# Global attention in a four-layer kernel: four turned buffers, the weights' chain four steps farther ahead, six groups of scores, pixels normalised three steps before their products

## The reference

```
h = group_norm(x, gn_scale, gn_bias)
hf = h.reshape(B, N, C)
q = hf @ wq + bq
k = hf @ wk + bk
...
w_ = jax.nn.softmax(w_, axis=2)
o = jnp.einsum('bqk,bkd->bqd', w_, v)
o = o @ wo + bo
return x + o.reshape(B, H, W, C)
```

## Time and profile before

| what | value |
|---|---|
| median of 3 runs | 3576.88 us (3575.83 to 3576.98) |
| the profiled execution | 3578.49 us, span 3576.7 us |
| PE busy over the span | 3127.8 us (87%) |
| ACT busy | 2605.6 us (73%) |
| layer 1, first to last PV | 738 to 2336 us |

### The profile page before, as it was taken

One profiled execution on the slowest core, in us unless ns is written; L12 is line 12 of the kernel. 1 busy time (PEld: TensorE's weight loads), 2 busy tenths in 40 slices (PEclk: granted clock), 3 DMA queues, 4 the chain that ended last, 5 costly groups with the idle time before them and its releaser, 6 DMA issues. The chain is left out here.

```text
span 3576.7 us, 62857 instructions
## 1 busy us (share of the span) xinstructions
PE 3127.8 (87%) x20468; PEld 2095.9 (59%) x20468; DVE 2731.2 (76%) x6707; ACT 2605.6 (73%) x4733; POOL 2184.7 (61%) x2044
## 2 busy tenths in 40 slices
PE   7999998599998999899998999877898857788898
PEld 5777776366655666565665666555666623333338
DVE  5899998566666666666666666568799979998888
ACT  4778887377877877777877778759676567776764
POOL 5789886155555665565555656643023458887885
PEclk8999999799999999999999999989999956878789
DMA  8777774189995999789996999942354455666559
GB/s 220 200 199 206 200 197 121 29 165 190 196 181 109 196 198 195 146 152 185 196 188 121 185 186 192 196 124 101 120 181 159 169 168 169 195 196 192 172 187 289
DMA packets 1327541, 623.51 MB, mean 174 GB/s; under 512 B 1105520, under 2 KB 1207536, under 8 KB 1326448
## 3 DMA queue, kind: packets, MB, share of 16 engines
q1 hardware_dynamic: 1296448, 551.83, 68.3%
q0 software_dynamic: 29184, 67.27, 7.1%
q10 hardware_dynamic: 1584, 0.40, 0.1%
HBM read 184.48 MB, written 113.25 MB: 83 GB/s over the span
## 5 line engine op out<-in xcount | busy, mean ns | idle before, releaser
L1115 POOL TENSOR_TENSOR l_halves<-l_pr,l_halves 128x1024 f16<-128x1024 f32 x384 | 833.1, 2182 | 549.7 <-ACT l_halves L948 546.9
L1076 DVE CUSTOM_DVE_ANT_0 l_pr<-l_S,l_zero 128x512 f32<-128x512 f32 x1024 | 671.8, 685 | 236.2 <-PE l_S L781 234.8
L948 ACT ACTIVATE l_halves<-l_pr 128x1024 f16<-128x1024 f32 x512 | 515.1, 1047 | 258.1 <-DMA l_turned<-l_halves 257.1
L943 ACT ACTIVATE l_pr<-l_pr,l_st,l_cols 128x1024 f32<-128x1024 f32 x512 | 628.0, 1227 | 10.6 <-DVE l_st L1082 10.6
L863 PE MATMUL l_O<-l_turned,l_vh 128*128 128x256 f16 x2048 | 564.1, 275 | 74.7 <-DMA l_turned<-l_halves 73.6
L864 PE MATMUL l_O<-l_turned,l_vl 128*128 128x256 f16 x2048 | 562.7, 275 | 0.0
L865 PE MATMUL l_O<-l_turned,l_vh 128*128 128x256 f16 x2048 | 562.5, 275 | 0.0
L779 PE MATMUL l_S<-l_kh,l_qh 128*128 128x512 f16 x1024 | 394.5, 385 | 11.4 <-DVE l_st L1076 11.4
L780 PE MATMUL l_S<-l_kh,l_ql 128*128 128x512 f16 x1024 | 392.8, 384 | 0.0
L781 PE MATMUL l_S<-l_kl,l_qh 128*128 128x512 f16 x1024 | 392.1, 383 | 0.0
L2196 POOL TENSOR_TENSOR l3b_du<-l3b_dt,l3b_u 128x512 f32<-128x512 f32 x256 | 329.6, 1288 | 102.1 <-DVE l3b_du L2108 80.5
(11 more groups left out here) (294 smaller groups left out, 7428.8 us busy)
## 6 DMA issues: line engine op xcount, KB each, us to landing
l3b_u<-ub SPq DMA_DIRECT2D x256, 256.0 KB, 3.0
l_kq<-l_hl SPq DMA_DIRECT2D x192, 128.0 KB, 5.4
l_kq<-l_hl POOLq DMA_DIRECT2D x192, 128.0 KB, 4.4
zs<-l_tmp SPq DMA_DIRECT2D x64, 256.0 KB, 3.3
ub<-l3a_u SPq DMA_DIRECT2D x32, 512.0 KB, 3.4
l3b_z<-zs SPq DMA_DIRECT2D x64, 256.0 KB, 3.7
yz<-l3b_z SPq DMA_DIRECT2D x64, 256.0 KB, 3.3
l3b_dt<-yz SPq DMA_DIRECT2D x32, 512.0 KB, 5.6
```

The source lines that it names most:

```text
L943: e.activation(unit, unit, ACT.Exp, bias=s[:, 9:10], scale=cols[:, 18:19], accum_out=s[:, 10 + m % 4:11 + m % 4]).then_inc(exped, 1)
L948: e.activation(halves[:, m % 2, 0, q, :], unit, ACT.Copy).then_inc(p_hi, 1)
L1076: e.tensor_tensor_reduce(pr[:, m % 7, q, 512 * (kc % 2):512 * (kc % 2) + 512], psS[:, bk, :], zero[:].broadcast_to([128, 512]), 1.0, -3.0e ...
L1115: e.tensor_tensor(halves[:, m % 2, 1, r, :], pr[:, m % 7, r, :], halves[:, m % 2, 0, r, :], ALU.subtract).then_inc(p_lo_pool, 1)
```

## The change

Five numbers move, and two of them are sizes of buffers:

- `LEAD` goes from 28 to 32: scores are made four steps earlier, and so is the first product of keys and queries, since its step is -LEAD - 3 from the start of the image. The products of the values stay where they are.
- ACT's exp and copy go from 11 to 15 steps ahead, the transposes and DVE's low halves from 8 to 12, POOL's low halves from 9 to 13.
- `turned` gets four groups instead of three (the transpose of m waits for PV of m - 4), `pr` six instead of seven (writing group m waits for the low halves of m - 6). `halves` keeps two.
- "normal" stands three steps before its product instead of two.
- What ends a round (L954, L876, L1122, L1100, L771) stays at its steps.

```diff
-        LEAD = 28
+        LEAD = 32
...
-        pr = P.sb("pr", [128, 7, 2, 1024])
+        pr = P.sb("pr", [128, 6, 2, 1024])
...
-        turned = P.sb("turned", [128, 3, 2, 2, 8, 128], F16)
+        turned = P.sb("turned", [128, 4, 2, 2, 8, 128], F16)
...
-                    plan(t - 2, "normal", b, ch, kind)
-                    plan(t - 4, "norm", b, ch, kind)
+                    plan(t - 3, "normal", b, ch, kind)
+                    plan(t - 5, "norm", b, ch, kind)
...
-                if m >= 3:
-                    w.wait_ge(pv_done, 4 * (m - 3) + 4)
+                if m >= 4:
+                    w.wait_ge(pv_done, 4 * (m - 4) + 4)
...
-                m, r = divmod(step + 8, 4)
+                m, r = divmod(step + 12, 4)
                 if 0 <= m < GROUPS and r % 2:
                     turn(m, r // 2)
...
-                m, r = divmod(step + 11, 4)
+                m, r = divmod(step + 15, 4)
...
-                    if m >= 7:
-                        low_halves(w, m - 7, q)
+                    if m >= 6:
+                        low_halves(w, m - 6, q)
...
-                m, r = divmod(step + 8, 4)
+                m, r = divmod(step + 12, 4)
                 if 0 <= m < GROUPS and r < 2 and on_vector(m, r):
...
-                m, r = divmod(step + 9, 4)
+                m, r = divmod(step + 13, 4)
                 if 0 <= m < GROUPS and r < 2 and not on_vector(m, r):
```

More of the change, by code:

```diff
@@ L614, in layer1 @@
         reach = psO[:, 0, 256:259]
-        p_turned = P.slots("p_turned", 3)
+        p_turned = P.slots("p_turned", 4)
         S_free = P.slots("S_free", 5)
@@ L672, in turned_in @@
         def turned_in(w, m):
-            w.wait_ge(p_turned[m % 3], 32 * (m // 3 + 1))
+            w.wait_ge(p_turned[m % 4], 32 * (m // 4 + 1))
         S_use, xc_use, count = {}, {}, {"stats": 0, "lo": 0, "hi": 0}
@@ L749, in turn @@
                     low_halves(w, m, 1)
-                e.dma_start(turned[:, m % 3, half].rearrange("p q k n -> p (q k) n"), halves[:, m % 2, half].rearrange("p q n -> p (q n)"), transpose=True).then_inc(p_turned[m % 3], 16)
+                e.dma_start(turned[:, m % 4, half].rearrange("p q k n -> p (q k) n"), halves[:, m % 2, half].rearrange("p q n -> p (q n)"), transpose=True).then_inc(p_turned[m % 4], 16)
             for step in steps:
@@ L861, in tensor @@
                         kt, at_k = 2 * j + k, 2 * (j % 4) + k
-                        hi, lo = turned[:, m % 3, 0, :, at_k, :], turned[:, m % 3, 1, :, at_k, :]
+                        hi, lo = turned[:, m % 4, 0, :, at_k, :], turned[:, m % 4, 1, :, at_k, :]
                         e.matmul(out, vh[:, kt, :], hi, start=(j == 0 and k == 0), stop=False)
@@ L936, in scalar @@
                         product(*a)
-                m, r = divmod(step + 11, 4)
+                m, r = divmod(step + 15, 4)
                 if 0 <= m < GROUPS:
-                    q, unit = r % 2, pr[:, m % 7, r % 2, :]
+                    q, unit = r % 2, pr[:, m % 6, r % 2, :]
                     if r < 2:
@@ L1073, in vector @@
                     w.wait_ge(S_full, u + 1)
-                    if m >= 7:
-                        low_halves(w, m - 7, q)
-                    e.tensor_tensor_reduce(pr[:, m % 7, q, 512 * (kc % 2):512 * (kc % 2) + 512], psS[:, bk, :], zero[:].broadcast_to([128, 512]), 1.0, -3.0e38,
+                    if m >= 6:
+                        low_halves(w, m - 6, q)
+                    e.tensor_tensor_reduce(pr[:, m % 6, q, 512 * (kc % 2):512 * (kc % 2) + 512], psS[:, bk, :], zero[:].broadcast_to([128, 512]), 1.0, -3.0e38,
                                            ALU.add, ALU.max, s[:, q, kc:kc + 1]).then_inc(S_free[bk], 1)
@@ L1082, in vector @@
                         e.tensor_scalar(s[:, :, 9:10], s[:, :, 8:9], cols[:, 19:20], LIFT, ALU.mult, ALU.add).then_inc(maxed, 1)
-                m, r = divmod(step + 8, 4)
+                m, r = divmod(step + 12, 4)
                 if 0 <= m < GROUPS and r < 2 and on_vector(m, r):
                     w.wait_ge(p_hi, 2 * m + r + 1)
-                    e.tensor_tensor(halves[:, m % 2, 1, r, :], pr[:, m % 7, r, :], halves[:, m % 2, 0, r, :], ALU.subtract).then_inc(p_lo_dve, 1)
+                    e.tensor_tensor(halves[:, m % 2, 1, r, :], pr[:, m % 6, r, :], halves[:, m % 2, 0, r, :], ALU.subtract).then_inc(p_lo_dve, 1)
                 if step % 16 == 3 and step > 16:
@@ L1111, in gpsimd @@
                         e.tensor_tensor(nl[:, z % 2, :], xc[:, i], f32(nh[:, z % 2, :]), ALU.subtract).then_inc(lo_done, 1)
-                m, r = divmod(step + 9, 4)
+                m, r = divmod(step + 13, 4)
                 if 0 <= m < GROUPS and r < 2 and not on_vector(m, r):
                     w.wait_ge(p_hi, 2 * m + r + 1)
-                    e.tensor_tensor(halves[:, m % 2, 1, r, :], pr[:, m % 7, r, :], halves[:, m % 2, 0, r, :], ALU.subtract).then_inc(p_lo_pool, 1)
+                    e.tensor_tensor(halves[:, m % 2, 1, r, :], pr[:, m % 6, r, :], halves[:, m % 2, 0, r, :], ALU.subtract).then_inc(p_lo_pool, 1)
                 if step % 16 == 3 and step > 16:
```

## The result

The changed kernel takes 3467.45 us (median of 4 runs, 3465.6 to 3474.96) against 3576.93 us before (4 runs, 3575.83 to 3577.03). The ratio is 0.9699, 95% interval 0.9682 to 0.9715: 109 us or 3.0% faster, where 87 us were forecast. The profiled executions have spans of 3464.0 and 3576.7 us, a difference of 112.7 us.

A forecast was written before the change was run, and what follows sets the result against it. PE was nearest to full, its idle time set by the copy, low halves, transpose chain in steady rounds and POOL's L1111 at products. Steady 31, products 33, start 18 and end 5 made 87 us: 3576.9 to 3490 us, range 3435 to 3550.

The forecast's parts named there:

- The steady part: Layer 1's steady rounds: the chain four steps earlier saves 0.6 us a round, 31 us over 52 rounds; bounds 0 and 73.7.
- the longest turn: Steady rounds: a `halves` buffer's cycle of copy, low halves, transpose, next copy sets the pace, shrinking from 11.6 to 10.9 us.
- a term I had put at nothing: Steady rounds: PE's wait for scores in DVE costs nothing while PE's five banks last, 6.5 us.
- rival B: Steady rounds: the fourth `turned` buffer closes all 73.7 us of PE's idle time; everything covered, 143 us, 3434 us; chance 0.12.
- The products: Three stretches before an image: normalising a step earlier takes back 11 of 14.2 us idle each, 33 us; bounds 0 and 43.
- ACT's 4.4 us: Product stretches: ACT's load for two steps and a product equals PE's own 4.4 us, so some PE waiting stays.
- The start: Before image 0: opening the products' serial dependence, less 2.6 us of added scores, gains 18 us net; bounds -3 and 23.
- The ring: Products: normalising the next one waits behind taking out the last; one step earlier opens this serial loop.
- The end: Last stretch of layer 1: fewer scores left and a chain farther ahead gain 5 us; bounds 0 and 14.
- A: Steady rounds: lead not used, `halves` sets the pace; only products, start and end gain, 3521 us; chance 0.20.
- C: Products gain little because ACT and DVE take POOL's place, and the steady part gains half: 3542 us; chance 0.10.
- D: Round ends: DVE's L1100 waits for the bias beyond 6.5 us, PE loses 2 us a round, 3630 us; chance 0.08.

The follow-up runs named there:

- e7: Kernel before with POOL's bias ahead of the low halves of the same step, nothing else: 3536.48 us, ratio 0.9885.
- e4: Kernel before with three groups in `halves` instead of two, paid for by `pr` with six: 3557.54 us, ratio 0.9949.
- e10: Changed kernel with POOL's bias ahead of the low halves and ACT's L954 ahead of its chain work in the step: 3465.02 us, ratio 0.9688.
- e11: e10 with L876, L1100 and the store four steps later, the bias left where it is: 3468.68 us, ratio 0.9702.
- e6: Changed kernel with the next image's pixels loaded ten steps earlier: 3462.73 us, ratio 0.9687.
- e12: e10 with the next image's pixels loaded ten steps earlier: 3465.29 us, ratio 0.9685.
- e9: Changed kernel with POOL's bias ahead of the low halves of its step: 3464.41 us, ratio 0.9687.
- e1: Kernel before with only the normalisation's step changed, pixels normalised three steps before their products: 3495.94 us, ratio 0.9778.
- e3: Kernel before with a fourth `turned` buffer and six groups of `pr`, no step moved: 3575.7 us, ratio 1.0000.
- e8: Changed kernel with three groups of `halves` and three of `turned`, in place of two and four: 3482.81 us, ratio 0.9739.

## Why the prediction was right, and where it was not

**The steady part** was right in place and size: 0.6 us a round forecast, 33.4 us in the 48 rounds cut out measured, 0.7 a round, and 1.1 in the round behind them. That DVE's stand behind POOL's bias was the cost is shown by e7, which takes the bias out of that queue and moves little else. A round takes 1093.3 / 48 = 22.8 us, 22.7 had been named.

**The sum behind that size did not hold**, so the size is in part luck. I let the longest turn of a `halves` buffer set the round. From ACT's first copy to the first copy of the group after next, averaged over the steady steps of all images, the turn of the round's last odd group fell from 12.3 to 10.8 us, where I had 8.0 plus queueing. That of the next even group fell from 12.4 to 11.9 (10.9 forecast), and that of the odd group behind rose from 11.1 to 12.2. So the longest turn shrank by 0.2 us, not by 0.7, while the round shrank by 0.7. A buffer is turned twice in a round, and a long turn can be followed by a short one. With a third buffer (e4) the round got 0.4 us shorter only. The low half of the odd group behind is 0.9 us late on average; I had worked out 1.5.

The second half of the cost was a term I had put at nothing: that PE's wait for scores in DVE costs nothing while a stand is under the 6.5 us of five banks. Before the change PE already waited 11.4 us for them in the steady steps, after stands of 3.7 to 5.1 us. In e7 that wait is gone, and PE's wait for the transposes fell by 9.1 us in the same steps, from 59.3 to 50.2.

**A step that failed** is the sign I named for rival B. PE's wait for the transposes did go altogether, and B was still wrong: its 73.7 us did not come. The wait went to another place. The stalls of PE over the steady steps, summed as what each step takes beyond 1.30 us, are 128 us before and 95 after. Before, 53 of them lie ahead of a round's last group, 24 ahead of its first and 26 at the one step with L876 (which has some 21 us of work of its own in them). Afterwards 62 lie at the step with L876, where PE waits for ACT's L954. I had listed the new waits on DVE and POOL and left out ACT's queue, where L954 now stands behind the copies of later groups. It cost nothing by itself, since in e10 and e11 this wait shrinks or goes without moving the time.

What sets the remaining 22.9 us a round in images 0 to 2 is open. In image 3, where no pixels are loaded for a next image of this layer, seven of the twelve steady rounds take 21.3 us. Loading earlier (e6, e12) did not bring that to the others, nor did the bias (e9) or the output (e10, e11). Moving the transposes of the pixels on PE (L789) was not tried. Nor was the likeliest rival: by the timeline of SP in the kernel after, the transposes, stores and loads in its queue add up to 258 of the 274 us of image 1's steady steps, 94%. Whether the queue is the limit or only fills the time that others leave it, no run here tells.

One round of image 3 takes 31.0 us (29.1 before). There SP issues thirteen loads for the next layer in a row, from 1953.1 to 1960.8 us in the kernel after, ahead of the transposes, and PE's longest wait for L954, 8.0 us, follows. The forecast doesn't treat it, and no run moves these loads.

**The products** were mis-sized: 33 us forecast, 48.2 measured, above my upper bound of 43. The mechanism was right, and e1 shows it alone, with 43.1 us. The three steady rounds in these stretches, at 0.7 us each, are some 2 us of the 48.2. The 32 steps before an image take 63.4 to 64.5 us, where I had named 74, though two of the sixteen products lie ahead of them now. Timeline of all engines in the kernel after, which answers to the earlier trace rows:

```profile
1052.56 1.28 DVE L998 TENSOR_SCALAR ahead<-l_xt,l_gs 128x512 f32<-128x512 f32 x1
...
1053.92 1.27 POOL L1111 TENSOR_TENSOR l_nl<-ahead,l_nh 128x512 fp32r<-128x512 f32 x1 [0.37 <-DVE ahead L998]
...
1054.37 0.74 DVE L1006 SCALAR_TENSOR_TENSOR l_kl<-l_S,l_cols,l_kh 128x512 f16<-128x512 f32 x1
...
1055.04 0.73 DVE L1006 SCALAR_TENSOR_TENSOR l_ql<-l_S,l_cols,l_qh 128x512 f16<-128x512 f32 x1
...
1055.55 0.48 PE L779 MATMUL l_S<-l_nh,l_wh 128*128 128x512 f32 x1
...
1057.03 0.39 PE L779 MATMUL l_S<-l_kh,l_qh 128*128 128x512 f16 x1
...
1059.57 0.48 PE L779 MATMUL l_S<-l_nh,l_wh 128*128 128x512 f32 x1
```

L1111 is done at 1055.19, and the product starts without a wait at 1055.55, while DVE still takes out the one before. Two errors made the term small. First, I took PE's own time for a product from its busy row, 1.8 us. From product to product it is 1059.57 - 1055.55 = 4.02 us, less two steps of 1.31 that is 1.4. The ends of matmuls are modelled, so the busy row probably counted some stalls as work. It fell by 4.1 us for practically the same instructions, of which the granted clock (0.97 and 0.98) explains a part, some 1.4 us by my estimate from these rows. So the 14.2 us of idle time were no ceiling: 14.6 to 17.0 us came back. Second, ACT's 4.4 us for two steps didn't bind. In one window in which every second step has a product of keys and queries, ACT is busy for 98% of the time and PE keeps its 4.0 us for a product and two steps:

```profile
1037.10:1061.20 24.10, 23.64 (x142) 16.05 (x140) 22.21 (x47) 23.60 (x35) 15.68 (x11) 1.00 0.66 124
```

ACT falls behind there and catches up where there are no products of keys and queries. With the lead the stretch gained only a little more (16.1 us on average) than without it (e1, 14.4).

**The start**: 18 us forecast, 23.3 measured, just above my bound of 23. PE's idle time fell from 25.8 to 7.2 us, so 18.6 of it came back; the other 5 us are busy time, which the clock probably shortened (see the last section). The ring alone gave 28.2 (e1). The kernels with the lead start 3.3 to 4.9 us slower than e1, where I had 2.6 for the added scores. **The end**: 5 forecast, 4.6 measured. PE's wait for L1111 was to fall under 20 us: counted from the first PV on, 43.3 us in 42 waits fell to 9.4 in 11, and with the start 72.6 to 20.4. The clock stayed at 0.99 to 1.00 in the steady steps.

**The rivals.** A (the lead not used) is refuted by the table. The steady part gained, as it also does without a lead in e7. For B, the Trainium skill, Perfetto Trace Analysis, section Optimization Strategy, says that a regular gap can mean a shortage of buffers. e3 adds the one in question and measures 1.0000 (0.9987 to 1.0013), so for `turned` the measurement decides against it; one more of `halves` gave 18 us (e4). A good part of the gap was a delay in a queue two engines away, and the fourth buffer helps only once something makes a lead (e8). C fell with ACT's load, which did not bind. D did not come as a loss. L1100 stands at most 4.3 us at a time for the bias after the change. But its mechanism is real and nearer than I put it: it costs PE 11.4 us before the change and 7.1 after it, from stands under 5.2 us, where I had 6.5 as the point at which it begins. Presumably not all five banks are free when DVE stops; that was not measured by itself.

## What to carry to other kernels

When an engine waits for a buffer, follow one turn of that buffer through every queue it passes before adding another: here one instruction behind an unrelated wait on a second engine cost 40 us, and the spare buffer at the place of the wait was worth nothing. Look at the banks in front of the stopped engine too: about half of that cost in the steady steps came through them. On POOL and DVE, work that ends a round belongs behind what the running chain needs next and ahead of what would make it wait; moving the chain or swapping two blocks did about the same here. And an operation that only prepares a later one should not stand in a queue behind the result of the previous one: one step earlier gave three quarters of all that was gained.

## What the runs showed of the hardware

The granted clock was probably part of the start's gain. Windows of the kernel before, then of the kernel after, from the first product on:

```profile
654.00:666.00 12.00, 6.70 (x15) 3.92 (x15) 4.37 (x7) 4.15 (x6) 1.95 (x3) 0.59 0.01 1
666.00:690.00 24.00, 16.68 (x55) 8.41 (x56) 12.83 (x30) 8.94 (x13) 5.95 (x5) 0.86 0.00 0
```

```profile
651.60:657.60 6.00, 5.97 (x15) 4.08 (x15) 2.71 (x4) 3.11 (x5) 2.20 (x2) 0.55 0.00 0
657.60:687.60 30.00, 28.43 (x139) 16.50 (x139) 28.09 (x68) 21.99 (x32) 12.47 (x10) 1.00 0.00 1
```

Both begin at the lower of the two levels, 1.2 GHz. With PE busy for 28.43 of the 30 us of the second window, the clock is at 2.4 GHz throughout it. In the kernel before, with PE idle for 30% of the 24 us of its second window, it is at 0.86 on average, going up and down. Behind the window shown it falls again in the kernel after too, to 0.78 over the last 24.5 us of the start, where PE is idle for 23%. The mean of the whole start rose from 0.80 to 0.87, and PE's busy time fell from 58.33 to 53.32 us although it had twelve instructions more. So a gap that is closed here seems to pay twice, which my term from idle time alone didn't have.

DVE's L1086 takes 1.22 us alone and up to 2.31 beside POOL's L1115 in the kernel after (3.19 in the kernel before): at 1192.03 it began while L1115 ran until 1193.26, and it ended 1.08 us after that, at 1194.34. The Trainium skill, SBUF — State Buffer, section SBUF: two separate sides, says that a VectorE operation with two inputs in SBUF contends with a GpSimd operation that reads SBUF for a shared pair of ports, and that the one which starts first keeps the pair for its whole instruction. This row agrees, and so do the other low halves of the kernel after that began while POOL was at work: all 102 ended 1.07 to 1.13 us after POOL's instruction. So a low half on DVE saves the chain less time than its 1.22 us would suggest.
